# An expert tile's activations turned by VectorE in 32x32 blocks, with the down product one tile later

## The reference

```python
logits = x @ gate_w                                  # 8 experts
top_v, top_i = jax.lax.top_k(logits, 2)
top_p = jax.nn.softmax(top_v, axis=-1)
g = einsum('th,ehi->tei', x, Wg)                     # 256 -> 704
u = einsum('th,ehi->tei', x, Wu)                     # 256 -> 704
d = einsum('tei,eih->teh', silu(g) * u, Wd)          # 704 -> 256
expert_out = einsum('te,teh->th', combine, d)        # weights top_p
shared = silu(x @ Sg) * (x @ Su) @ Sd
x = x + layernorm(expert_out + shared)
```

## Time and profile before

| what | value |
|---|---|
| median of 3 runs | 1816.83 us |
| profiled execution, its own time | 1820.9 us |
| its span, first to last instruction | 1819.1 us |
| scan stage, up to the first turn of rows | 1187 us |
| expert stage, up to the last scatter's start | 1187 to 1779 us |
| TensorE busy | 1600.4 us, 88% of the span |
| VectorE busy | 1157.1 us, 64% |
| POOL busy | 1039.3 us, 57% |
| ScalarE busy | 854.4 us, 47% |

### The profile page before, as it was taken

The page is one execution under the profiler, slowest core; times in us unless marked ns, Lnnn a source line. Parts: engine busy times, 40 slices in busy tenths (PEclk is TensorE's granted clock), DMA queues, the critical chain, the costliest instruction groups (busy, mean ns, idle before and its releaser), DMA issues.

```text
span 1819.1 us, 23416 instructions
## 1 busy us (share of the span) xinstructions
PE 1600.4 (88%) x6828; PEld 1037.3 (57%) x6828; DVE 1157.1 (64%) x1928; ACT 854.4 (47%) x1480; POOL 1039.3 (57%) x1225
## 2 busy tenths in 40 slices
PE   5888798898998898998898768699999999999990
PEld 2344455655555555645555545467677777777770
DVE  2299898898898898998898997222222222222225
ACT  3566657657657657657657554222112121221214
POOL 0578769769778779778779885312222222222224
PEclk9899999999999999999999978799999999999995
DMA  3111112211211211211211752514212221212215
GB/s 96 48 35 48 47 41 74 77 41 48 77 46 45 74 47 46 77 43 51 69 46 47 217 155 70 175 42 109 47 33 33 34 33 33 33 33 35 33 29 191
DMA packets 84393, 116.19 MB, mean 64 GB/s; under 512 B 11121, under 2 KB 58577, under 8 KB 84273
## 3 DMA queue, kind: packets, MB, share of 16 engines
q1 hardware_dynamic: 63344, 82.94, 14.7%
q0 software_dynamic: 16704, 27.57, 7.7%
q10 hardware_dynamic: 4224, 4.19, 0.7%
HBM read 81.05 MB, written 33.10 MB: 63 GB/s over the span
## 4 chain that ended last, share of the span: by engine, by line
PE 37%; DVE 4%; POOL 4%; issue 4%; ACT 2%; DMA 1%; POOLq 0%; DVEq 0%; ACTq 0%; SPq 0%
PE A L1241 10%; PE bA L1200 9%; PE bH L1200 9%; POOL arena L1005 2%; DVE arena L853 2%; PE bY L1224 2%; PE bH L589 1%; DVE arena_t L870 1%; DMA sum_scratch<-arena_t 1%; PE A L1232 1%; PE A L1224 1%; PE A L470 1%; PE A L519 1%; PE A L552 1%; PE A L574 1%
## 5 line engine op out<-in xcount | busy, mean ns | idle before, releaser
L1005 POOL TENSOR_TENSOR arena<-arena 128x512 f32<-128x512 f32 x512 | 645.9, 1274 | 184.7 <-DVE arena L853 182.0
L727 ACT ACTIVATE bA<-arena,a_neg 128x512 f32<-128x512 f32 x512 | 353.4, 692 | 282.8 <-DVE arena L853 277.7
L589 PEld LDWEIGHTS bH<-ident,arena 128*128 128x128 f32 x2048 | 256.8, 147 | 298.9 <-issue 158.0
L589 PE MATMUL bH<-ident,arena 128*128 128x128 f32 x2048 | 327.4, 286 | 69.1 <-DVE arena L853 57.0
L853 DVE TENSOR_TENSOR_SCAN arena<-bA,arena 128x512 f32<-128x512 f32 x256 | 306.9, 1214 | 44.7 <-ACT bA L727 32.4
L853 DVE TENSOR_TENSOR_SCAN arena<-bA,hl,arena 128x512 f32<-128x512 f32 x256 | 323.3, 1276 | 16.0 <-ACT bA L727 16.0
L1336 POOL DMA_INDIRECT sum_scratch<-arena_t x71 | 113.5, 1598 | 188.5 <-issue 160.3
L1372 ACT ACTIVATE arena_t<-bA 128x352 f32<-128x352 f32 x142 | 58.1, 461 | 324.0 <-PE bA L1200 324.0
L1241 PE MATMUL A<-arena,hT 128*128 x852 | 197.5, 382 | 0.8 <-ACT hT L1378 0.8
L1330 POOL DMA_DIRECT2D arena_t<-expert_in_scratch x71 | 40.6, 572 | 257.9 <-PE A L1232 201.7
L1200 PE MATMUL bA<-arena,arena_t 128*128 x568 | 179.8, 459 | 1.3 <-ACT arena_t L1383 1.3
(11 more groups left out here) (190 smaller groups left out, 2084.8 us busy)
## 6 DMA issues: line engine op xcount, KB each, us to landing
arena<-b_scratch SPq DMA_DIRECT2D x128, 256.0 KB, 3.2
arena_t<-expert_in_scratch POOLq DMA_DIRECT2D x71, 132.0 KB, 2.4
arena<-in_L_ffn_Wg_dram SPq DMA_DIRECT2D x8, 704.0 KB, 6.2
arena<-in_L_ffn_Wu_dram SPq DMA_DIRECT2D x8, 704.0 KB, 7.8
arena<-in_L_ffn_Wd_dram SPq DMA_DIRECT2D x8, 640.0 KB, 8.4
arena<-in_L_attn_x_dram SPq DMA_DIRECT2D x8, 512.0 KB, 5.0
arena_x<-in_L_attn_x_dram SPq DMA_DIRECT2D x8, 512.0 KB, 5.0
x_scratch<-arena_x SPq DMA_DIRECT2D x8, 512.0 KB, 3.4
```

The source lines that it names most:

```text
L589: i = e.transpose(bH[g % NH][:, q * P:(q + 1) * P], hh[:, (n - 1) % 2, q, d * P:(d + 1) * P], ident[:])
L727: e.activation(bA[g % NA][:], dt[c % 2][:, d, :], ACT.Exp, scale=a_neg[:, d, n:n + 1]).then_inc(s_a, 1)
L1005: e.tensor_tensor(bb[:, k % NB, :], u[c % 2][:, d, :], br[:, n % NR, :], ALU.mult).then_inc(s_bb, 1)
```

## The change

TensorE no longer turns the activations. VectorE does it in blocks of 32 x 32 (dve_turn): per tile 16 instructions, one for each pair of a 32-partition group of hm (a) and a 32-partition group of hT (q). Each reads 32 tokens and every fourth block of 32 columns, six blocks for q = 0, 1 and five for q = 2, 3, and writes each turned block to its place in hT. The banks bHA, bHB and the copies out of them are gone; the down product has two banks in turn. The down product and its result move one tile later (t-2 in the loop of t), the row places grow from 4 to 5, the weights' from 2 to 3. In TensorE's program the read of the expert's number for the down product now stands right before that product.

```diff
-NF, NB4, NX = len(FIT), 4, 4
+NF, NX, NHT, BLK, NG = len(FIT), 5, 2, 32, 3
...
-    bX, bG, bU, bHA, bHB, bD = A[0], bA, bH, bY, A[1], A[2]
+    bX, bG, bU, bD = A[0], bA, bH, [A[1], A[2]]
...
     def pe_down(e, t, ex):
-        e.wait_ge(s_ka, t + 1)
-        e.wait_ge(s_kb, t + 1)
-        if t:
-            e.wait_ge(s_yt, t)
+        e.wait_ge(s_th, t + 1)
+        if t >= 2:
+            e.wait_ge(s_yt, t - 1)
...
+    def dve_turn(e, t):
+        e.wait_ge(s_h, t + 1)
+        if t >= NHT:
+            e.wait_ge(s_dn, t - NHT + 1)
+        for q in range(P // BLK):
+            n = (FI // BLK - q + P // BLK - 1) // (P // BLK)
+            for a in range(P // BLK):
+                i = e.transpose(hT[q * BLK:(q + 1) * BLK, t % NHT, 0:n, a * BLK:(a + 1) * BLK],
+                                hm[a * BLK:(a + 1) * BLK, t % 2, :].rearrange("p (b i) -> p b i", i=BLK)[:, q::P // BLK, :])
+        i.then_inc(s_th, 1)
...
     def pool_tiles(e):
...
                     e.wait_ge(s_ys, 16 * (n + 1 - NX))
                 row = e.value_load(tab[0:1, 1, n:n + 1], min_val=0, max_val=SPARE + (E - 1) * P)
                 e.dma_start(xt[:, n % NX, :], xs_d[bass.ds(row, P), :]).then_inc(s_in[n % NX], 16)
-            if t >= 1:
-                e.wait_ge(s_in[(t - 1) % NX], 16 * ((t - 1) // NX + 1))
-                e.wait_ge(s_yt, t)
+            if t >= 2:
+                m = t - 2
+                e.wait_ge(s_in[m % NX], 16 * (m // NX + 1))
+                e.wait_ge(s_yt, m + 1)
...
     def pe_tiles(e):
...
-            if t:
-                pe_turn_h(e, t - 1)
-            if t < NT:
                 pe_up(e, t, ex)
             if t + 1 < NT:
                 pe_turn_in(e, t + 1)
-            if t:
-                pe_down(e, t - 1, last)
+            if t >= 2:
+                pe_down(e, t - 2, pe_expert(e, t - 2))
...
     def dve_tiles(e):
...
                 i.then_inc(s_h, 1)
-            if t:
-                e.wait_ge(s_dn, t)
+                dve_turn(e, t)
+            if t >= 2:
+                e.wait_ge(s_dn, t - 1)
...
-                e.tensor_scalar(yt[:, (t - 1) % 2, :], bD[:, 0:DM], gt[:, (t - 1) % 2:(t - 1) % 2 + 1], None, ALU.mult).then_inc(s_yt, 1)
+                e.tensor_scalar(yt[:, t % 2, :], bD[t % 2][:, 0:DM], gt[:, (t - 2) % NG:(t - 2) % NG + 1], None, ALU.mult).then_inc(s_yt, 1)
```

More of the change, by code:

```diff
@@ L180, in program @@
     bT = take(CH)[0:2 * NS]
-    arena_t = sb("arena_t", [P, 2 * ND * CH + ND * DM])
+    arena_t = sb("arena_t", [P, NX * RW + 2 * (KD * P + 2 * FI + DM)])
     take = places(arena_t)
@@ L1166, in dve_scans @@
                     table_tiles(e)
-    hT = sb("hT", [P, 2, NF, P])
-    gt = sb("gt", [P, 2])
-    bX, bG, bU, bHA, bHB, bD = A[0], bA, bH, bY, A[1], A[2]
+    hT = sb("hT", [P, NHT, NF, P])
+    gt = sb("gt", [P, NG])
+    bX, bG, bU, bD = A[0], bA, bH, [A[1], A[2]]
     s_wt = sem("s_wt")
@@ L1176, in program @@
     s_tx = sem("s_tx"); s_kx = sem("s_kx"); s_g = sem("s_g"); s_gu = sem("s_gu"); s_si = sem("s_si"); s_h = sem("s_h")
-    s_th = sem("s_th"); s_ka = sem("s_ka"); s_kb = sem("s_kb"); s_dn = sem("s_dn"); s_yt = sem("s_yt"); s_ys = sem("s_ys")
+    s_th = sem("s_th"); s_dn = sem("s_dn"); s_yt = sem("s_yt"); s_ys = sem("s_ys")
     acc = arena[:, 0:NU * UT * DM].rearrange("p (u j d) -> p u j d", u=NU, j=UT)
@@ L1215, in pe_up @@
         pe_inner(e, ex, t, KD * FI, bU, s_gu)
-    def pe_turn_h(e, t):
-        e.wait_ge(s_h, t + 1)
-        if t:
[L1220 to L1225, removed]
     def pe_turn_in(e, t):
@@ L1235, in pe_down @@
     def pe_down(e, t, ex):
-        e.wait_ge(s_ka, t + 1)
-        e.wait_ge(s_kb, t + 1)
-        if t:
-            e.wait_ge(s_yt, t)
+        e.wait_ge(s_th, t + 1)
+        if t >= 2:
+            e.wait_ge(s_yt, t - 1)
         for q in range(NF):
-            i = e.matmul(bD[:, 0:DM], hT[:, t % 2, q, :], arena[:, bass.ds(ex * EW + (2 * KD * FI + q * DM), DM)],
+            i = e.matmul(bD[t % 2][:, 0:DM], hT[:, t % NHT, q, :], arena[:, bass.ds(ex * EW + (2 * KD * FI + q * DM), DM)],
                          start=(q == 0), stop=(q == NF - 1))
         i.then_inc(s_dn, 1)
+    def dve_turn(e, t):
[8 more added lines that the diff above has]
+        i.then_inc(s_th, 1)
     def dve_gate(e, t):
         x_ = xt[:, t % NX, :]
-        g = gt[:, t % 2:t % 2 + 1]
+        g = gt[:, t % NG:t % NG + 1]
         e.wait_ge(s_in[t % NX], 16 * (t // NX + 1))
-        if t >= 2:
-            e.wait_ge(s_yt, t - 1)
+        if t >= NG:
+            e.wait_ge(s_yt, t - NG + 1)
         e.tensor_scalar(g, x_[:, I1:I1 + 1], te[:, t:t + 1], x_[:, P1:P1 + 1], ALU.is_equal, ALU.mult).then_inc(s_gm, 1)
@@ L1319, in pool_tiles @@
         e.wait_ge(s_sc, 16 * J * TOPK * NCH)
-        for t in range(-2, NT + 1):
-            if t == 1:
+        for t in range(-2, NT + 2):
+            if t == 2:
                 e.wait_ge(s_shs, 16 * NCH)
@@ L1330, in pool_tiles @@
                 e.dma_start(xt[:, n % NX, :], xs_d[bass.ds(row, P), :]).then_inc(s_in[n % NX], 16)
-            if t >= 1:
-                e.wait_ge(s_in[(t - 1) % NX], 16 * ((t - 1) // NX + 1))
-                e.wait_ge(s_yt, t)
[L1334 to L1337, removed]
+            if t >= 2:
+                m = t - 2
+                e.wait_ge(s_in[m % NX], 16 * (m // NX + 1))
+                e.wait_ge(s_yt, m + 1)
+                if m:
+                    e.wait_ge(s_ys, 16 * m)
+                e.indirect_dma_start(out=sh_d, out_offset=bass.IndirectOffsetOnAxis(ap=xt[:].bitcast(U32)[:, m % NX, TOK:TOK + 1], axis=0),
+                                     in_=yt[:, m % 2, :], in_offset=None, compute_op=ALU.add).then_inc(s_ys, 16)
         for u in range(NU):
@@ L1345, in pe_tiles @@
         pe_turn_in(e, 0)
-        ex = None
-        for t in range(NT + 1):
-            last = ex
+        for t in range(NT + 2):
             if t < NT:
                 ex = pe_expert(e, t)
-                if t:
-                    last = pe_expert(e, t - 1)
                 pe_gate(e, t, ex)
-            elif t:
-                last = pe_expert(e, t - 1)
-            if t:
-                pe_turn_h(e, t - 1)
-            if t < NT:
                 pe_up(e, t, ex)
@@ L1373, in act_tiles @@
                 i.then_inc(s_si, 1)
[L1374 to L1378, removed]
             if t + 1 < NT:
@@ L1410, in dve_tiles @@
                 i.then_inc(s_h, 1)
-            if t:
-                e.wait_ge(s_dn, t)
-                if t >= 3:
-                    e.wait_ge(s_ys, 16 * (t - 2))
-                e.wait_ge(s_gt, t)
-                e.tensor_scalar(yt[:, (t - 1) % 2, :], bD[:, 0:DM], gt[:, (t - 1) % 2:(t - 1) % 2 + 1], None, ALU.mult).then_inc(s_yt, 1)
+                dve_turn(e, t)
+            if t >= 2:
+                e.wait_ge(s_dn, t - 1)
+                if t >= 4:
+                    e.wait_ge(s_ys, 16 * (t - 3))
+                e.wait_ge(s_gt, t - 1)
+                e.tensor_scalar(yt[:, t % 2, :], bD[t % 2][:, 0:DM], gt[:, (t - 2) % NG:(t - 2) % NG + 1], None, ALU.mult).then_inc(s_yt, 1)
         for u in range(NU + 2):
```

## The result

The changed kernel is slower: 1956.39 us, the median of four runs (1948.9 to 1962.25), against 1817.63 of before in the same session. The ratio is 1.076, interval 1.072 to 1.079. I had forecast 1874 with a range up to 1910. The direction was right, the size was not: +139 us in place of +57. The profiled execution took 1962.25 us with a span of 1960.5, 141 longer than before.

What follows compares the result with a forecast made beforehand. TensorE bounds the kernel before; after the change a two-tile loop of rows, 8.86 us per tile, was to bind. Loop +44, end +10 and burst 3 sum to +57 us: 1874 us, range 1820 to 1910.

Steps and rivals of the forecast that it cites:

- What bounds the kernel before, and TensorE's floor: Expert stage: TensorE, without gaps, sets 8.20 us per tile; without turns of the activations its floor is 7.55.
- The loop of rows: Down product, 16 turns, result, scatter, row load, turn of rows, next down product: 17.7 us for two tiles.
- The 16 turns at 5.4 us: VectorE's block turns per tile: 339 ns each without overlap, 5.4 us in all; lower bound 4.05.
- The bare table read, 0.55 us: TensorE's read of the expert's number between turn of rows and down product: 0.55 us, lower bound 0.
- The sum per tile, 8.86 us: Expert stage: the loop gives 8.86 us per tile against 8.20, +44 us for 66 tiles.
- 1.3 us of stand per tile: TensorE waits about 1.3 us for rows ahead of each turn of rows.
- the clock falls in the gaps: Rival: TensorE drops to 1.2 GHz in a quarter of the tiles, +14 us, 1888; its share lies within the forecast's 0.65.
- The end and the burst: Last scatters of the stage +10 us; row loads slowed while x1 is loaded near 1271, +3 us (0 to 8).

Runs made afterwards that it cites:

- result-first kernel: Changed kernel with VectorE writing the result of tile t-2 ahead of the 16 block turns of tile t, not behind them: 1788.8 us, ratio 0.982.
- the pairs: Kernel with the result ahead of the turns, each of the 16 block turns cut in two on the same 32-partition groups: 1850.4 us, ratio 1.016.
- early-read kernel: Changed kernel with the read of the expert's number for the down product moved ahead of the turn of rows: 1914.8 us, ratio 1.051.
- the two kernels with a fill: Unused TensorE matmuls per tile: two added to the changed kernel, 1916.3 us; one added to the kernel with the table read ahead of the turn of rows, 1888.6 us.
- the kernel with two fills: Changed kernel with two unused matmuls of the gate product's shape after each up product on TensorE: 1916.3 us, ratio 1.051.

## Why the prediction was right or wrong

*What bounds the kernel before, and TensorE's floor:* right. (VectorE's row falls already at slice 26 and TensorE's is solid from slice 27, not 28 and 29; nothing rests on it.) The floor of 7.55 us per tile was reached by the result-first kernel at 7.54.

*The loop of rows:* right in each of its links, shown by cutting it at two places (1789 and 1810 us) and by leaving the turns and the bare read out of it (1826). The later down product and the fifth place alone are harmless.

*The 16 turns at 5.4 us:* right in the choice (no overlap, shown by the pairs), 0.45 us too short. A turn of 192 elements is 368 ns and one of 160 is 338, so 0.94 ns per element over a fixed part of 188 between these two sizes, where I had 1.02 over 160 from the two-input product.

*The bare table read, 0.55 us:* 0.6 by the early-read kernel.

*The sum per tile, 8.86 us:* wrong, and the step that failed is in its term "down product 2.59": the loop was summed at the full clock, with "1.3 us of stand per tile" spread evenly. In the profiled pair the down product in the loop took 4.14 us, and 31 of 68 ran at the low clock. I took a loop over two tiles for half of it in each tile. There are two such loops, one through the even tiles and one through the odd ones, and TensorE takes them in order. When one of them is late it pushes the other back, which then has its rows in time and does not stand. VectorE's own 7.87 us hold the short tile at 7.9 (from result to result) and all the rest of the pair, some 12.3 us, falls on the other. Its stand is 2.5 us and not 1.3; behind it the clock is low, as after the stand of 2.7 us near 1276; and the slowed down product lies in the very loop that sets the pace, 1.55 us in this pair. Unevenness alone would have cost nothing: the sum of a pair is the loop either way, as the early-read kernel shows. My rival "the clock falls in the gaps" had the cause but a price of 14 us: I let the clock fall in a quarter of the tiles, and it fell in nearly half; and I shared the loss of each over two tiles, while it fell on the late loop each time. Without the low clock the loop of 20.1 us would be 18.6, 9.29 per tile, and by my own sum 1902 us, inside the range; that is an estimate, borne out by the two kernels with a fill, which kept the clock and gained.

The error in numbers: the loop is 20.1 us against 17.7. Of the 2.4, 1.55 are the clock, 0.48 the turns, 0.19 the row load behind the scatter (5.25 for 5.06), 0.12 the release and 0.10 the table read, less 0.03 in the result. Per tile that is 1.2 us, over 68 tiles 82 us, the distance between +57 and +139. How the first unevenness arises wasn't tried by itself. In the trace the first stand is already 4.6 us long (at 1223.9), before the two loops have settled. Why the clock stayed up behind some stands of 2.2 to 2.8 us and fell behind others of the same length is open too.

*The end and the burst:* by the spacing of the scatters, the first comes 11.4 us later than before (1215.5 for 1204.0) and the last two intervals give 3.6 us back: +8 where I had +10. The two intervals around the burst sum to 27.9 us, 7.8 over a usual pair, against 4.7 over two usual tiles before: +3, as forecast.

## What to carry to other kernels

When work moves to an engine with idle time, ask which result stands behind it in that engine's order, and follow that result to what it releases; here a 0.5 us instruction behind 5.9 us of turns held back a scatter, a row load and TensorE, and exchanging the two turned a loss of 8% into a gain of 2%. A loop that closes over two tiles need not share its slack evenly: look at consecutive tiles one by one, not at the mean, and price the longest stand, since the clock behind it can be a part of the loop. Work of no use, put where TensorE stood, made this kernel 40 us faster; that is a test of the clock and not a cure.

## What the runs showed of the hardware

A turn of 32x32 blocks in float32 on 32 partitions took 368 ns for 192 elements of a partition and 338 for 160. A straight line through these two (0.94 ns per element over 188) does not hold for the pairs: there 96 elements took 255 to 274 ns as the first of a pair and some 225 as the second, where the line gives 278, and 64 took 195 as the second, where it gives 248. Turns from or to other partitions than the one ahead didn't overlap with it (13 ns between them); with the same partitions they did, by some 65 ns.

The granted clock was low behind 31 of the 33 stands of some 2 us and more in the changed kernel, a stage where TensorE was otherwise busy. In the early-read kernel of 24 stands of 2.1 us and more 13 brought it down and 11, of 2.2 to 2.8 us, did not, so the length of the stand alone doesn't decide. In the expert stage it never fell behind a stand of up to 1.3 us in any run here; the shortest that brought it down was 1.37 us, with the bare read of 0.5 us behind it (1582.92 in the kernel with two fills).

VectorE at 96% busy, with turns from SBUF to SBUF, left the scatter's instruction on POOL at 1.60 us and its landing at 3.9 us (3.8 before).
